# GpSimd makes the first scaled one-hot of every second column in the sort of the first chunk of edges

## What is computed

```
xn  = layernorm(x)
agg = segment_sum(xn[dst], src, num_segments=6250)      # row dst of xn is added to node src
cnt = segment_sum(ones, src, num_segments=6250)
x   = x + xn @ W1.T + b1 + (agg / max(cnt, 1)) @ W2.T + b2 + linear_attention_mix(xn)
x   = x + mixture_of_experts(layernorm(x))              # 8 experts, capacity 1280, hidden 1024
```

## Time and profile before

| | us |
|---|---|
| median of 3 runs | 2270.8 (2270.57 to 2271.77) |
| the profiled execution, its own time | 2270.43 |
| its span in the trace | 2268.8 |
| VectorE busy in the span | 1531.5 (68%) |
| TensorE (PE) busy | 1494.6 (66%) |
| GpSimd (POOL) busy | 1087.1 (48%) |
| ScalarE (ACT) busy | 738.0 (33%) |
| the first chunk's sort, from its first one-hot to its last product | 191.2 to about 373 |

### The profile page before, as it was taken

How to read it: one execution, slowest core, us unless ns; L and a number is a source line. 1 busy time by engine, 2 the same in 40 slices (tenths; PEclk the granted TensorE clock), 3 DMA queues, 4 the chain that set the end, 5 groups by cost and what they waited for, 6 DMA issues and landing times. The chain is left out here.

```text
span 2268.8 us, 27209 instructions
## 1 busy us (share of the span) xinstructions
PE 1494.6 (66%) x6201; PEld 784.8 (35%) x6201; DVE 1531.5 (68%) x4280; ACT 738.0 (33%) x2080; POOL 1087.1 (48%) x1045
## 2 busy tenths in 40 slices
PE   0005886444577777765555556666487399999997
PEld 0001332100122222222222233333276266666665
DVE  8979998899888888876566654444377244444444
ACT  1235995000377777600000001111176222222221
POOL 2010002777777666677777777777435311111111
PEclk9999998555699999955555567766597599999999
DMA  4126001333333322733333333336744412222310
GB/s 139 37 77 285 0 0 31 99 91 91 93 100 102 89 79 80 76 109 102 103 104 105 104 103 98 100 98 90 121 142 161 151 53 85 93 96 100 99 60 5
DMA packets 89284, 212.69 MB, mean 94 GB/s; under 512 B 20226, under 2 KB 49448, under 8 KB 86192
## 3 DMA queue, kind: packets, MB, share of 16 engines
q0 software_dynamic: 52656, 140.17, 23.7%
q1 hardware_dynamic: 34840, 70.56, 9.1%
q10 hardware_dynamic: 1680, 0.67, 0.1%
HBM read 166.08 MB, written 49.89 MB: 95 GB/s over the span
## 5 line engine op out<-in xcount | busy, mean ns | idle before, releaser
L709 DVE TENSOR_TENSOR XA<-XA,bank 128x257 f32 x896 | 376.6, 420 | 358.7 <-PE bank L519 337.3
L380 POOL DMA_INDIRECT G<-xn_parts,idx x448 | 449.8, 1004 | 339.4 <-DVE srcl L781 165.6
L498 PE MATMUL bank<-HT,LV 125*128 125x496 f16 (+1 forms) x1600 | 401.5, 359 | 245.5 <-DVE HT L860 145.9
L444 ACT ACTIVATE LV<-LH,v 125x128 f16<-125x128 f16 x1490 | 449.5, 387 | 341.1 <-DVE LH L907 309.3
L380 POOL DMA_INDIRECT w<-xn_parts,idx x448 | 467.6, 1044 | 136.5 <-issue 136.5
L518 PE MATMUL bank<-G,S 128*128 128x257 f16 x448 | 158.0, 353 | 216.9 <-DMA G<-xn_parts,idx 161.6
L498 PEld LDWEIGHTS bank<-HT,LV 125*128 125x128 f16 x1600 | 117.7, 98 | 465.3 <-DVE HT L860 220.9
L518 PE MATMUL bank<-w,S 128*128 128x257 f16 x448 | 157.9, 352 | 164.6 <-DMA w<-xn_parts,idx 139.6
L1502 POOL DMA_INDIRECT out<-ob,tok x64 | 66.1, 1033 | 402.6 <-DVE ob L1488 402.6
L1426 PE MATMUL bank<-w,ht 128*117 128x256 f32 (+1 forms) x1024 | 223.7, 379 | 0.0
L1415 PE MATMUL bank<-xt,w 128*128 128x468 f32 (+1 forms) x512 | 215.5, 579 | 0.8 <-ACT xt L1440 0.8
(11 more groups left out here) (219 smaller groups left out, 2022.0 us busy)
## 6 DMA issues: line engine op xcount, KB each, us to landing
w<-f SPq DMA_DIRECT2D x16, 1024.0 KB, 7.8
expert_rows<-G SPq DMA_DIRECT2D x7, 2048.0 KB, 19.4
xb<-expert_rows SPq DMA_DIRECT2D x8, 1028.0 KB, 11.1
xb<-expert_rows SPq DMA_DIRECT2D x8, 939.7 KB
G<-xn_parts,idx POOLq DMA_INDIRECT x448, 2.8
w<-xn_parts,idx POOLq DMA_INDIRECT x448, 2.8
XA<-x SPq DMA_DIRECT2D x6, 1024.0 KB, 5.2
xn_parts<-G POOLq DMA_DIRECT2D x12, 512.0 KB, 3.8
```

The source lines that it names most:

```text
L380: pool.indirect_dma_start(g[:, o:o + 2 * D], None, tab, bass.IndirectOffsetOnAxis(ap=idx[:, t:t + 1], axis=0)).then_inc(s_g[t % RING], 16)
L444: ins = act.activation(LV[0:EP, (2 * q + n) * P:(2 * q + n + 1) * P], LH[0:EP, q * P:(q + 1) * P], ACT.Copy, scale=v[0:EP, ds(col, 1)])
L498: ins = pe.matmul(psV[n][:, 0:tiles], LV[0:EP, (2 * q + n) * P:(2 * q + n + 1) * P], HT[0:EP, q * TMAX:q * TMAX + tiles], start=False, sto ...
L709: v.tensor_tensor(XA[:, ds(o, AGW)], XA[:, ds(o, AGW)], psA[t % AR][:, 0:AGW], ALU.add).then_inc(s_ev, 1)
```

## The change

`VSHARE` becomes 2. Where VectorE made the `v1` piece of every third column of a round, GpSimd now makes that of every second one (columns 1, 3, 5, ... 15), by multiplying `LH` with `v1`; ScalarE makes the `v1` piece of the other columns and all `v2` pieces as before. VectorE makes none, and no longer copies `v1` to `here`. GpSimd's 176 instructions stand in its list behind the wait for the zeros and the setting of `G`'s ones, ahead of the gathers; each waits for its own column of `LH`. TensorE waits before each odd column for GpSimd's piece.

```diff
-VSHARE = 3
+VSHARE = 2
...
+    s_lp = sem("lane_values_by_pool")
...
         pool.memset(G[:, 2 * D:GR * GW:GW], 1.0).then_inc(s_one, 1)
         pool.wait_ge(s_one, 2)
+        for col in range(COLS0):
+            q = col % KR
+            if col % CU % VSHARE == VSHARE - 1:
+                pool.wait_ge(s_lh, col + 1)
+                pool.tensor_scalar(LV[0:EP, 2 * q * P:(2 * q + 1) * P], LH[0:EP, q * P:(q + 1) * P],
+                                   v1[0:EP, col:col + 1], None, ALU.mult).then_inc(s_lp, 1)
         for t in range(TILES):
...
                 if j % CW == 0:
                     pe.wait_ge(s_lv, col + CW)
                     pe.wait_ge(s_ht, col + (CW + GR))
+                if j % VSHARE == VSHARE - 1:
+                    pe.wait_ge(s_lp, i * (CU // VSHARE) + (j // VSHARE + 1))
                 column(col, j % KR, CHUNKS[0][3])
...
-        def sort(i, tiles=T0, share=VSHARE):
+        def sort(i, tiles=T0):
             v.wait_ge(s_ht, i * CU + GR)
             v.tensor_copy(posh[0:EP, :], pos[0:EP, ds(i * CU, CU)])
-            v.tensor_copy(v1h[0:EP, :], v1[0:EP, ds(i * CU, CU)])
             v.tensor_copy(tfh[0:EP, :], tf[0:EP, ds(i * CU, CU)]).then_inc(s_posh, 1)
...
-                for n in range(j, j + CW):
-
-                    if n % share != share - 1:
-                        continue
-                    q = n % KR
-                    v.tensor_scalar(LV[0:EP, 2 * q * P:(2 * q + 1) * P], iota_t[0:EP, 0:P],
-                                    posh[0:EP, n:n + 1], v1h[0:EP, n:n + 1], ALU.is_equal, ALU.mult)
```

## The result

| | us |
|---|---|
| changed kernel, median of 5 runs | 2282.3 (2277.9 to 2283.7) |
| kernel before on the same chip, median of 5 | 2270.8 (2269.5 to 2272.4) |
| ratio, with its 95% interval | 1.0045 (1.003 to 1.006): 7 to 14 us slower |
| its profiled execution, own time; span | 2279.5; 2277.9 |
| first gather, first lane one-hot | 380.89 (before 377.57), 191.10 |

What follows compares the result with a forecast made beforehand. VectorE was taken to set the sort's 8.19 us round. Standstill 19.3 + slow restart 1.0 + longer rounds 9.0 - sort's end 0.5 = +28.8 us on 2270.4, forecast 2299.5 us, range 2277 to 2330.

Steps and rivals of the forecast that it cites:

- What bounds: In the sort, VectorE sets the 8.19 us round, ScalarE 0.2 us behind; VectorE's share without the moved work is 6.97.
- The stop, 19.3 us: At the sort's start, VectorE stands still from 194.84 to 214.1 because GpSimd's products wait for the zeros: 19.3 us lost.
- The 1.0 for a second slow start: After the standstill early in the sort, TensorE starts slowly a second time, with seven columns queued: 1.0 us added.
- d = 0.205 us per product, rounds of 8.61, +9.0 us: In sort rounds, each 0.37 us GpSimd product blocks VectorE for 0.35, of which 0.145 is hidden; 8 products a round.
- The first rival: In the sort, short products hide in VectorE's gaps: rounds of 7.2 us, gain offset by the starting standstill, 2269; 8%.
- my case: The main forecast for sort rounds: d, VectorE's loss per GpSimd product, from 0.11 to 0.30 us, total 2284 to 2315; 62%.
- Behind decode everything should only be later by the same amount: Behind the sort, decode and all gathers shift by the sort's delay alone, with no cost of their own.
- end of the sort: At the last pair ScalarE has no backlog, shortening VectorE's 2.35 us wait for TensorE by perhaps 0.5 us.

Runs made afterwards that it cites:

- run 4: The kernel before, with TensorE waiting once, before column 1, until GpSimd is past the zeros, and no product moved: ratio 1.0085, 22 us slower.
- 6: The changed kernel again, unedited, on a chip where the kernel before takes 2395 us: ratio 1.0019, 4.8 us slower.
- 11: The changed kernel plus an iota on GpSimd between the last product and the first gather: ratio 1.0018 to the kernel before, 3.1 us slower.
- 12: The changed kernel again, unedited, on a chip where the kernel before takes 2271.0 us: ratio 1.0038, 8.4 us slower.
- 2: The changed kernel without GpSimd's products, odd columns' v1 pieces left zero: rounds of 6.99 us, first gather at 352.28; nothing behind the sort is read.
- 7: The kernel before again, unedited, against itself on a chip where it takes 2395 us: ratio 0.9999, rounds of 8.19 us.
- 8: The kernel before plus one single spare GpSimd product ahead of the wait for the zeros: ratio 1.0011, 2.5 us slower by the ratio.
- run 3: The kernel before plus 176 spare GpSimd products that nobody reads, ahead of the wait for the zeros: ratio 1.0019, 4.6 us slower, rounds of 8.59 us.
- 9: The changed kernel with products moved ahead of the wait for the zeros and an iota behind them: ratio 0.9940 to the kernel before, 13.9 us faster.
- 10: The changed kernel with products moved ahead of the wait for the zeros, without an iota: ratio 0.9956 to the kernel before, 11.0 us faster.
- 5: The kernel before plus 176 spare GpSimd memsets of 125x128 f16 that nobody reads, one per odd column: ratio 1.0004, rounds of 8.21 us.
- run 1: The changed kernel with GpSimd's products moved ahead of its wait for the zeros: ratio 0.9917, 2368.9 us against 2388.4 for the kernel before.

## Why the prediction was wrong

- **What bounds**: right. VectorE alone would need 6.97 us a round; without products it took 6.99.
- **The stop, 19.3 us**: right, 18.4 (17.8 at the first gather of run 4, which has the stop alone). The zeros landed 1.2 us earlier than in the trace of before, so VectorE went on at 213.2 and not at 214.1. That they land earlier goes with the stop: the memset behind them ends at 211.5 to 211.8 in the changed kernel's profile and in those of runs 4, 6, 11 and 12, and at 212.7 to 213.0 in those of runs 2, 7 and 8. The 1.0 for a second slow start was not seen: from the ninth to the seventeenth column VectorE took 4.95 us, against 5.08 before.
- **The step that failed: d = 0.205 us per product, rounds of 8.61, +9.0 us.** Measured 0.066, rounds of 7.52, -14.4 us: an error of 23 us. The error has two parts, and they partly offset each other. The length, 0.37 from the middle of two GpSimd rows, is 0.73 in the mean; it lay outside both, above 0.45, which was meant as the upper one. The share that VectorE feels, all of the length but 0.02 us and 0.145 us hidden, came from a memset of 16 elements and from a cast that stood still for 10.8 us. The durations were read rightly. But a memset that was hidden whole shows only that 0.14 us can be hidden, not that no more can, and an instruction of GpSimd's that lasts 0.73 us does not shut VectorE out for 0.73 us. If it did, run 3's round would have been 14 us; it was 8.59. By the rule of the Trainium skill that I cited (SBUF — State Buffer, Who interferes with whom), the loser is blocked for the whole instruction. In its length as the profile shows it the product contradicts this: 0.73 us long, 0.066 felt. That the lock covers only the part in which data moves would fit the memsets, the cast and the add, but no run here separates the parts. With this step the first gather was forecast for 406; it started at 380.9.
- **The first rival** (port free enough, 7.2 us, 2269) was nearer in the sort but did not hold either: its break-even, 7.27 us a round by a total of 19.8, lies under the measured 7.52, and the gather did start late. The measured d of 0.066 lies in the band between it and my case (0.04 to 0.11), to which I gave 8%. Its other condition, a short product, fails as well: the first two products of the changed kernel took 0.61 and 0.59 us before VectorE went on at 213.21. By the Trainium skill's line rate (GPSIMD Engine Reference, Engine selection) 128 elements would be an estimated 0.11 us. The trace does not agree with it for this shape. Only one size was run, so whether the rate is lower or a fixed part comes on top is not shown.
- **"Behind decode everything should only be later by the same amount"**: wrong, and this is the term that was missing from the sum. After the products each later gather takes 11 ns longer to issue, some 5.4 us in all where GpSimd sets the gathers' pace (runs 11 and 12; runs 9 and 10 differ by 2.9, which is not clear of the scatter).
- With the measured sizes the sum for the first chip's profile is 18.4 - 14.4 - 0.7 (end of the sort and the rest) = 3.3 at the first gather, + 5.8 behind it: 9.1. The median, 11.5, has 2.4 more, within what single runs of the changed kernel differ by (2277.9 to 2283.7). That the total lies in my range is luck: with d = 0.066 my own sum gives rounds of 7.50 us and 2275, below the range. Two errors of opposite sign met in it, -23 us in the sort's rounds and +6 (profiles) to +8 (medians) behind the sort.

## What to carry to other kernels

Work that is handed to an engine with a straight list starts when the list gets there: look what that engine waits for ahead of it, and put the new work in front of the wait. Moved ahead, the same 176 instructions turned a loss of 8 to 12 us into a gain of 11 where before takes 2270 us, and a loss of 4.8 into a gain of 19.5 where it takes about 2390 (loss and gain were measured on different chips of a kind). One iota behind the products took off 5.3 us in the changed kernel; behind the moved products the 2.9 us that it gained are not clear of the scatter. A rate measured where two engines exclude each other for one long instruction says little of many short ones: measure it with spare instructions in the kernel before.

## What was not expected of the hardware

- A GpSimd tensor_scalar of 125x128 f16 lasts 0.59 us with VectorE standing still, 0.73 beside VectorE in the changed kernel (0.76 in the median), 0.90 in the median in run 3; a memset of the same size takes 0.20.
- VectorE loses 0.05 to 0.07 us to each such product and 0.003 to 0.006 to each memset.
- After one GpSimd tensor_scalar each issue of an indirect DMA on GpSimd takes 957 ns instead of 946, for the 1.2 ms that follow; an iota in between undoes it, a memset doesn't. The numbers repeat to 1 ns in the result, in runs 5 to 7 and in 8 to 10, and with 3 ns more in the others but for run 1. Why is open: I ran only iota and memset as the instruction behind, and only tensor_scalar as the cause.
